# Two layers of a transformer kernel with another order of each engine's work

## The reference

```python
q = rmsnorm(x @ Wq + bq, qn_w)            # per head
k = rmsnorm(ctx @ Wk + bk, kn_w)          # per head
v = ctx @ Wv + bv
p = softmax(q @ k.T * scale + mask)
out = (p @ v) @ Wo
```

```python
q, k, v = linear_fp8(x, wq), linear_fp8(x, wk), linear_fp8(x, wv)   # own
qx = linear_fp8(x, wqx)                                            # asks the context
kx, vx = split(ctx @ w_kv_x)
q, k, qx, kx = (layernorm per head of each)
core = softmax(q @ k.T * scale) @ v
xout = softmax(qx @ kx.T * scale) @ vx
out = round_fp8(concat(core, xout) / smooth) @ wproj
```

## Time and profile before

| | us |
|---|---|
| median of three runs | 4422.85 (4418.86 to 4425.76) |
| the profiled execution | 4422.6 |
| its span, first to last instruction | 4420.8 |
| `l2x`, tiles 0 to 6 | 392.7 |
| `l2x`, last tile | 47.6 |
| `l3x`, one period | 97.5 |

### The profile page before, as it was taken

How to read it: one execution, slowest core, us unless ns; L and a number is a source line. 1 busy time by engine, 2 the same in 40 slices (tenths; PEclk the granted TensorE clock), 3 DMA queues, 4 the chain that set the end, 5 groups by cost and what they waited for, 6 DMA issues and landing times. The chain is left out here.

```text
span 4420.8 us, 69997 instructions
## 1 busy us (share of the span) xinstructions
PE 3591.5 (81%) x26672; PEld 2566.4 (58%) x26672; DVE 2633.6 (60%) x5418; ACT 1722.9 (39%) x3305; POOL 361.6 (8%) x566
## 2 busy tenths in 40 slices
PE   7999998997787887753888776878888886878778
PEld 4655557876764555531555643535555555757667
DVE  6888885443367777876444363247667665453552
ACT  4888883111344343421333212224444442223323
POOL 3000000000000000000111000111111111121000
PEclk8555558998886666756988788989999997989787
DMA  2000001000010000010000014000000001200000
GB/s 78 1 0 0 0 0 72 0 0 19 7 36 20 0 0 0 0 58 2 5 5 5 5 59 134 0 3 3 3 5 3 3 3 35 82 0 0 1 1 10
DMA packets 44826, 72.66 MB, mean 16 GB/s; under 512 B 25805, under 2 KB 33489, under 8 KB 41045
## 3 DMA queue, kind: packets, MB, share of 16 engines
q1 hardware_dynamic: 36440, 70.54, 4.6%
q10 hardware_dynamic: 8256, 0.52, 0.2%
HBM read 67.91 MB, written 3.15 MB: 16 GB/s over the span
## 5 line engine op out<-in xcount | busy, mean ns | idle before, releaser
L1316 DVE TENSOR_SCALAR_CACHE_REDUCE l0x_ex<-l0x_s_ps 128x1024 f32<-128x1024 f32 x258 | 305.6, 1222 | 63.4 <-PE l0x_s_ps L1019 62.4
L1151 ACT ACTIVATE l0x_ex<-l0x_ex,l0x_neg_max,l0x_q_scale 128x2048 f32<-128x2048 f32 x128 | 267.9, 2093 | 52.4 <-DVE l0x_neg_max L1322 50.7
L1031 PEld LDWEIGHTS l0x_t_ps<-l0x_identb,l0x_pb 128*128 128x128 bf16 x2048 | 200.0, 142 | 109.4 <-issue 56.8
L1019 PE MATMUL l0x_s_ps<-l0x_kT,l0x_qT 64*128 64x512 bf16 x516 | 235.5, 600 | 32.9 <-ACT l0x_qT L1146 19.5
L1158 ACT ACTIVATE l0x_pt<-l0x_t_ps 128x1024 bf16<-128x1024 bf16 x256 | 246.3, 1014 | 32.2 <-PE l0x_t_ps L1031 32.2
L1031 PE MATMUL l0x_t_ps<-l0x_identb,l0x_pb 128*128 128x128 bf16 x2048 | 233.7, 304 | 6.8 <-ACT l0x_pt L1158 4.1
L1331 DVE TENSOR_SCALAR l0x_pb<-l0x_ex 128x2048 bf16<-128x2048 f32 x128 | 156.4, 1222 | 0.0
L263 PE MATMUL l3x_bank<-l3x_wproj,l3x_cat 128*128 128x256 f32 x512 | 120.7, 390 | 32.1 <-DVE l3x_cat L3345 32.1
L263 PE MATMUL l3x_bank<-l3x_w_kv_x,l3x_ctxT 128*128 128x512 f32 x256 | 129.8, 655 | 0.9 <-ACT l3x_ctx_q L762 0.9
L263 PEld LDWEIGHTS l3x_bank<-l3x_wproj,l3x_cat 128*128 128x128 f32 x512 | 96.1, 193 | 52.4 <-DVE l3x_cat L3345 38.7
L1019 PEld LDWEIGHTS l0x_s_ps<-l0x_kT,l0x_qT 64*128 64x128 bf16 x516 | 50.0, 121 | 129.4 <-issue 80.4
(11 more groups left out here) (740 smaller groups left out, 8651.6 us busy)
## 6 DMA issues: line engine op xcount, KB each, us to landing
l3x_wproj<-in_L_xattn_wproj SPq DMA_DIRECT2D x1, 4096.0 KB, 22.5
l3a_w<-in_L_attn_W SPq DMA_DIRECT2D x4, 1024.0 KB, 11.4
l2f_w<-in_L_ffn_w SPq DMA_DIRECT2D x1, 2816.0 KB, 12.4
l0x_ctxT<-in_ctxT SPq DMA_DIRECT2D x8, 256.0 KB, 3.0
l0a_wq<-in_L_attn_W_Q SPq DMA_DIRECT2D x1, 2048.0 KB
l0a_wk<-in_L_attn_W_K SPq DMA_DIRECT2D x1, 2048.0 KB
l0a_wv<-in_L_attn_W_V SPq DMA_DIRECT2D x1, 2048.0 KB, 8.0
l0a_wo<-in_L_attn_W_O SPq DMA_DIRECT2D x1, 2048.0 KB, 13.0
```

Source lines behind the costliest of these rows:

```text
L1019: ins = mm(s_ps[:, j * 512:(j + 1) * 512], qT[rows, h // 2, :], kT[rows, h // 2, j * 512:(j + 1) * 512], start=True, stop=True)
L1031: ins = nc.tensor.transpose(t_ps[:, j * P:(j + 1) * P], pb[:, h % 2, j * P:(j + 1) * P], identb[:])
L1151: s.activation(ex[:, h % 4, :], ex[:, h % 4, :], ACT.Exp, scale=q_scale[:, h:h + 1], bias=nb[:, h:h + 1], accum_out=sums[:, h:h + 1]).then ...
L1316: v.tensor_scalar(ex[:, h % 4, c], s_ps[:, c], 1.0, None, ALU.mult, ALU.max, accum_out=mx[:, h, half:half + 1]).then_inc(o.up(scores_taken ...
```

## The change

In both layers instructions change their places in the queues of TensorE, ScalarE, VectorE and GpSimd. None is added or removed. In `l2x` the first `mix` moves ahead of the turning of `q0`, the copies of turned probabilities ahead of the normalising that stood before them, and on VectorE `weigh(0)` ahead of `shift(1)` and the statistics of the queries ahead of `weigh(1)` and of `take_out(0)`. In `l3x` the opening of a tile becomes a function `begin`, called once before the loop and then for the next tile between the last two products; the loop's body now begins with turning `x0`. `x0.stats_of` and `own.shift` are likewise done for the first tile ahead of VectorE's loop, and for the next tile ahead of `add_out`. Within the period fills of the context's keys and values move ahead of `mix` and `turn` of the own attention, and the first product behind `cross.score(0)`.

```diff
--- before.py
+++ after.py
@@ -2759,8 +2759,9 @@
                 if more:
                     free(kk, t + 1)
                     q1.fill(pe, t + 1)
+                att.mix(pe, t, 0)
+                if more:
                     q0.turn(pe, t + 1)
-                att.mix(pe, t, 0)
 
                 att.turn(pe, t, 1)
                 if more:
@@ -2793,21 +2794,22 @@
                     whole(norm.scalar(o, ln_bank))
                     kk.normalise(o)
                     o.t = t
-                att.exponential(o, 1)
                 if more:
                     o.t = t + 1
                     kk.take(o)
-
+                    o.t = t
+                att.exponential(o, 1)
+                att.take_turned(o, 0)
+                if more:
+                    o.t = t + 1
                     q0.normalise(o)
+                    q0.take(o)
                     o.t = t
-                att.take_turned(o, 0)
+                att.take_turned(o, 1)
                 if more:
                     o.t = t + 1
-                    q0.take(o)
-
                     q1.normalise(o)
                     o.t = t
-                att.take_turned(o, 1)
                 act.wait_ge(att.out_ps.sem, att.out_ps.value(t))
                 if more:
                     o.t = t + 1
@@ -2879,18 +2881,18 @@
                     whole(normalising)
                     kk.stats_of(o)
                     o.t = t
+                att.weigh(o, 0)
                 att.shift(o, 1)
-                att.weigh(o, 0)
-                att.weigh(o, 1)
                 if more:
                     o.t = t + 1
                     q0.stats_of(o)
                     o.t = t
-                att.take_out(o, 0)
+                att.weigh(o, 1)
                 if more:
                     o.t = t + 1
                     q1.stats_of(o)
                     o.t = t
+                att.take_out(o, 0)
                 att.take_out(o, 1)
                 dve.wait_ge(y_ps.sem, y_ps.value(t))
                 v.tensor_tensor(xt, xt, y_bank, ALU.add).then_inc(o.up(tile_done), 1)
@@ -3445,43 +3447,45 @@
             free(sq0, 0)
             sv.fill(pe, 0)
             sq1.turn(pe, 0)
-            def tile(t, more):
+
+            def begin(t):
                 free(sq1, t)
                 x0.fill(pe, t)
                 pe.wait_ge(cross.out_taken.sem, cross.out_taken.value(t, 0))
                 own.score(pe, t, 0)
-
                 free(sv, t)
                 x1.fill(pe, t)
+
+            begin(0)
+            def tile(t, more):
                 x0.turn(pe, t)
-                if more:
-                    whole(ln.tensor(pe, t + 1, ln_bank))
-
                 free(x0, t)
                 pe.wait_ge(ctx_loaded.sem, ctx_loaded.value(t))
                 kc0.fill(pe, t)
                 if more:
+                    whole(ln.tensor(pe, t + 1, ln_bank))
+                x1.turn(pe, t)
+                if more:
                     pe.wait_ge(ln.ready.sem, ln.ready.value(t + 1))
                 pe.wait_ge(tile_done.sem, tile_done.value(t, 0))
                 own.turn(pe, t, 0)
-                x1.turn(pe, t)
-                own.mix(pe, t, 0)
 
                 free(x1, t)
                 kc1.fill(pe, t)
+                own.mix(pe, t, 0)
                 own.turn(pe, t, 1)
                 kc0.turn(pe, t)
-                own.mix(pe, t, 1)
 
                 free(kc0, t)
                 vc0.fill(pe, t)
+                own.mix(pe, t, 1)
                 kc1.turn(pe, t)
-                part_of_y(t, 0)
 
                 free(kc1, t)
                 vc1.fill(pe, t)
                 pe.wait_ge(own.out_taken.sem, own.out_taken.value(t))
                 cross.score(pe, t, 0)
+                part_of_y(t, 0)
 
                 free(vc0, t)
                 if more:
@@ -3512,6 +3516,8 @@
                     sv.fill(pe, t + 1)
                     sq1.turn(pe, t + 1)
                 part_of_y(t, 2)
+                if more:
+                    begin(t + 1)
                 part_of_y(t, 3).then_inc(y_ps.sem, 1)
             with pe.Fori(0, TILES - 1) as t:
                 tile(t, True)
@@ -3528,18 +3534,17 @@
             sv.take(first)
             def tile(t, more):
                 o = Order(act, L.order["act"], t)
-                own.exponential(o, 0)
-
                 x0.normalise(o)
                 x0.take(o)
+                own.exponential(o, 0)
+
+                x1.normalise(o)
                 if more:
                     o.t = t + 1
                     whole(ln.scalar(o, ln_bank, scale=ln_w, bias=ln_b))
                     o.t = t
-
-                x1.normalise(o)
+                x1.take(o)
                 own.take_turned(o, 0)
-                x1.take(o)
 
                 kc0.normalise(o)
                 own.take_turned(o, 1)
@@ -3592,9 +3597,12 @@
                 if more:
                     o.t = t + 1
                     whole(norm.pool(o))
+                    o.t = t
+                x1.invert(o)
+                if more:
+                    o.t = t + 1
                     whole(ln.pool(o))
                     o.t = t
-                x1.invert(o)
                 kc0.invert(o)
                 kc1.invert(o)
                 if more:
@@ -3657,15 +3665,16 @@
             round_inputs(first)
             for phase in (sk, sq0, sq1):
                 phase.stats_of(first)
+            x0.stats_of(first)
+            own.shift(first, 0)
             def tile(t, more):
                 o = Order(dve, L.order["dve"], t)
-                x0.stats_of(o)
                 if more:
                     o.t = t + 1
                     first_norm, second_norm = norm.vector(o, tile_of(env.x, t + 1)), ln.vector(o, norm.y[:])
                     next(first_norm)
                     o.t = t
-                own.shift(o, 0)
+                x1.stats_of(o)
                 if more:
                     o.t = t + 1
                     whole(first_norm)
@@ -3677,16 +3686,13 @@
                     whole(second_norm)
                     o.t = t
 
-                x1.stats_of(o)
+                kc0.stats_of(o)
                 if more:
                     o.t = t + 1
                     round_inputs(o)
                     o.t = t
-
-                kc0.stats_of(o)
+                kc1.stats_of(o)
                 own.take_out(o, 0)
-
-                kc1.stats_of(o)
                 own.take_out(o, 1)
                 dve.wait_ge(own.out_taken.sem, own.out_taken.value(t, 1))
                 round_heads(o, 0)
@@ -3718,6 +3724,11 @@
                 round_heads(o, 0)
                 dve.wait_ge(cross.out_taken.sem, cross.out_taken.value(t, 2))
                 round_heads(o, 1)
+                if more:
+                    o.t = t + 1
+                    x0.stats_of(o)
+                    own.shift(o, 0)
+                    o.t = t
                 dve.wait_ge(y_ps.sem, y_ps.value(t))
                 add_out(o, tile_done)
                 dve.wait_ge(o.sem, o.at())
```

More of the change, by code:

```diff
@@ L2799, in tile @@
                     kk.take(o)
-                    q0.normalise(o)
                     o.t = t
+                att.exponential(o, 1)
                 att.take_turned(o, 0)
@@ L2805, in tile @@
                     o.t = t + 1
+                    q0.normalise(o)
                     q0.take(o)
+                    o.t = t
+                att.take_turned(o, 1)
+                if more:
+                    o.t = t + 1
                     q1.normalise(o)
                     o.t = t
-                att.take_turned(o, 1)
                 act.wait_ge(att.out_ps.sem, att.out_ps.value(t))
```

## The result

Four runs of the changed kernel took 4273.82 us in the median (4268.19 to 4278.6), beside 4423.5 us (4418.86 to 4425.76) for the kernel before on the same chip: a ratio of 0.966, with a 95% interval of 0.9644 to 0.9675. The forecast was 4305 with a range of 4281 to 4350.

What follows compares the result with a forecast made beforehand. TensorE's own work was taken as the bound underneath, with waits and slow clock on top. From 4422.6 us, -98.7 in `l2x` and -19 in `l3x` gave 4305, range 4281 to 4350.

Steps and rivals of the forecast that it cites:

- the waits of 1.88 and 4.53: In each `l2x` period, TensorE's waits in us before `att.turn(0)` and `att.mix(1)`, forecast to go.
- the margins ahead of `mix(0)` and `mix(1)`: In `l2x`, time in hand before the two products start, forecast at 1.3 and 2.5 us.
- The last tile: In `l2x`, the tile with no next one to prepare: left at 47.6 us, between -4 and +2.
- Rival 4: In `l2x`, full clock not granted to a TensorE that never pauses: +181 us, 4585; chance 0.04.
- Rival 2: In `l2x`, one queue comes late after all: 25 us (4330) or 63 us (4368); chance 0.14.
- The jump's stall: In `l3x`, 4.7 us a period after VectorE's jump to the loop's head, taken as gone because the head moves past a block's edge.
- the new waits for `kc0.take` and `kc1.take`: In `l3x`, new TensorE waits before `vc0.fill` and `vc1.fill`: 1.7 and 1.2 us a period.
- the term for the clock: In `l3x`, clock expected to fall after the 5.1 us wait as before: 5 us a period kept, 5.3 in the sum.
- The ends of `l3x`: In `l3x`, the first tile, whose jump never stalled, -3 us and the last -2.
- Rival 1: In `l3x`, the loop's stall stays, on the way to the norm: 99.8 us a period, total 4335; chance 0.17.
- Rival 3: In `l3x`, the norm's wait shorter and the clock kept: 92.5 us a period, total 4288; chance 0.08.
- bound of -40 for `l3x`: The `l3x` gain's far bound in us, with clock loss and the wait for the norm both half.

Runs made afterwards that it cites:

- e8: The changed kernel with VectorE's queue of `l2x` put back as before, TensorE and ScalarE as after: 4298.76 us, ratio 0.9719.
- e3: The kernel before with ten small VectorE memsets in front of the `l3x` loop and nothing else changed: 4402.0 us, ratio 0.9947.
- e4: The changed kernel with 97 small VectorE memsets in front of the `l3x` loop: 4279.78 us, ratio 0.9678.
- e7: The changed kernel with 109 small VectorE memsets in front of the `l3x` loop: 4301.0 us, ratio 0.9721.
- e10: The changed kernel with `x1`'s statistics ahead of `add_out`, `own.weigh(0)` behind the norm's `y`, and `x1.turn`, `x1.take`, `kc1.fill` earlier in `l3x`: 4267.58 us, ratio 0.9643.
- e11: e10 with TensorE's wait for the norm's copies moved behind `kc1.fill` in its `l3x` queue: 4265.07 us, ratio 0.9654.
- e6: The changed kernel with TensorE's queue of `l2x` put back (`q0.turn` ahead of `mix(0)`), VectorE and ScalarE as after: 4320.71 us, ratio 0.9769.

## Why the prediction was right in its waits and wrong in its size

**`l2x`, -98.7 forecast, -110.1 measured.** Each step held: the waits of 1.88 and 4.53 gone, the margins ahead of `mix(0)` and `mix(1)` 1.5 and 2.5 us for 1.3 and 2.5, only the gaps ahead of the norm's turning and of the output product left, clock 1.00. The term was mis-sized: 42 us taken where 41.6 had been worked out and 40.93 came (gaps 0.95 for 1.2, work 40.0 for 40.3), 7.7 us over the first seven tiles. The last tile, left at 47.6 with bounds of -4 and +2, took 43.9. Rival 4, a clock not granted to a TensorE without pauses, is refuted by the 1.00 over 286 us. Rival 2 did not happen, but its price, 25 us for a gap of 1.88, is near what e8 showed for a gap of 1.9: 22 us in the layer.

**`l3x`, -19 forecast, -38.2 measured: the step that failed.** The jump's stall went for the reason given. e3, e4 and e7 show that the place decides, under both orders. `y` came 9.96 us after the sum for 10.0, TensorE's wait was 4.7 for 5.1, the new waits for `kc0.take` and `kc1.take` together 2.7 for 2.9, for `x0.take` 1.2 for 1.0. All waits add to 12.0, forecast 12.4. What failed is the term for the clock, "I keep its 5 us", 5.3 in the sum. It made 77.4 + 5.3 = 82.7 us of TensorE time, and it was 79.98. That is 2.7 of the 3.1 us by which 95.1 missed 92.0, and six periods of 3.1 are 18.6 us, nearly the whole difference of the layer.

The runs show two faults in that term. First, it was not consistent: before, the clock fell twice a period, for 6.7 us behind the 5.7 us wait and for 3.5 us behind the waits of 1.6 and 0.74 at 3184. The forecast removed these later waits from the sum and kept the slow clock that followed them. After, there is one slow stretch. Second, the term was made as period x (1 - clock), which counts slow time in which TensorE had nothing to do. What the slow clock costs is read from the same matmuls at either clock. The slow stretch of the changed kernel:

```profile
3149.22 0.69 PE L241 MATMUL l3x_bank<-ident,l3x_ln_y 128*128 128x128 f32 x2 [4.72 <-DVE l3x_ln_y L213]
3149.70 1.91 PE L707 MATMUL l3x_bank<-ident,l3x_rows 128*128 128x128 f32 x8
3151.41 1.91 PE L821 MATMUL l3x_bank<-ident,l3x_pb 128*128 128x128 f32 x8
3153.11 4.58 PE L263 MATMUL l3x_bank<-l3x_w_kv_x,l3x_ctxT 128*128 128x512 f32 x8
```

The same work in e10 at a clock of 1.00:

```profile
3238.27 1.04 PE L707 MATMUL l3x_bank<-ident,l3x_rows 128*128 128x128 f32 x8
3239.14 0.38 PE L241 MATMUL l3x_bank<-ident,l3x_ln_y 128*128 128x128 f32 x2
3241.30 3.67 PE L263 MATMUL l3x_bank<-l3x_w_kv_x,l3x_ctxT 128*128 128x512 f32 x8 [1.77 <-ACT l3x_ln_yT L255]
```

And in the kernel before, a fill in the first slow stretch, the wait of 1.6, and the `mix` in the second slow stretch:

```profile
3176.90 4.94 PE L263 MATMUL l3x_bank<-l3x_w_kv_x,l3x_ctxT 128*128 128x512 f32 x8
...
3184.31 0.66 PE L707 MATMUL l3x_bank<-ident,l3x_rows 128*128 128x128 f32 x4 [1.60 <-ACT l3x_rows L755]
...
3186.68 3.54 PE L831 MATMUL l3x_bank<-l3x_pt,l3x_own_v 128*128 128x128 f32 x16 [0.32 <-ACT l3x_pt L845]
```

The four groups of the changed kernel take 9.1 us for 6.1 at full clock (the turning of the probabilities takes 1.04 there, like that of the rows). So the slow clock cost about 3.0 us after, and its work is 77.0, near the 77.4 of the forecast: of the 5.3 about 3.0 came. Before, the same way of counting gives 4.1 (with two turnings of 1.12 for 0.66, and 1.95 for this `mix` at full clock), not 4.9. In e7 the clock of the period is 0.95, as before, and TensorE is busy for 79.09: the first three groups take the same time as above, but `kc1.fill` is back at 3.69, so some 2.1 us were lost where 95.58 x 0.05 gives 4.8. Most of the slow stretch lay in the 9.2 us wait.

**The ends of `l3x`** gave -6.7 us together, forecast -5. **Rival 1**, the stall stays, is e7: 95.6 a period and 4301, where the rival said 99.8 and 4335; it had the mechanism, but kept the same clock term. **Rival 3** had the number for a period, 92.5, by a way that was half right: less was lost to the clock, but the wait for the norm was no shorter (4.7). The rule of the Trainium skill (Runtime: NRT & Kernel Launch, Instruction fetch mechanics), two blocks of 256 instructions, and a taken branch out of them stalls, is borne out in its second half by e7. Its blocks are not: the packets here were 8 KB (5 packets, 0.04 MB), 128 instructions apart, and a body of some 269 stayed loaded in e3, e4 and after. How many instructions stay loaded in all was not measured. The reading of it that this loop stalls wherever it lies is refuted.

**What no step had:** `l3a` took 4.7 us more (361.0 for 356.3), by its clock; its instructions are the same. It did so too with the `l3x` part alone (361.0) and with e3's ten memsets (360.4), but not with the `l2x` part alone (356.6) nor in e11 (356.6), and in e4 it took 364.6. So it is not the new order of `l3x` alone that brings it. Why the clock fell otherwise was not tried and stays open.

So -117.7 forecast, and 11.4 more in `l2x`, 19.2 more in `l3x`, 4.7 given back in `l3a`: 143.6 of the profiled executions' 144.0. The medians are 149.7 apart; the 6 us between lie within the scatter of the changed kernel's executions, 4268.19 to 4278.6. Neither miss alone would have left the range: 4422.6 - 110.1 - 19 is 4293.5, and 4422.6 - 98.7 - 38.2 is 4285.7. The forecast's own bound of -40 for `l3x` held; its range had no room for a gain in `l2x` beside it.

Some sums of the prediction are slightly off, and nothing hangs on them: its rows give 4.9 for the clock where it adds 5.3, 40.3 + 1.2 is 41.5, and in rival 1 15 less 5 is 10, not 11. Its 3.42 us of stall after the sum was not all stall either, as e3 shows: 1.15 of it is a wait for `x0.fill` that stays in the old order.

## What to carry to other kernels

When a wait is taken out of a sum, take out the slow clock behind it as well, and price the clock from the same matmuls in a slow stretch and at full clock, not from the mean clock of a period. Before a stall at a loop's jump is laid to the order of the work, put a few idle instructions in front of the loop, in more than one number: if it goes, it is a matter of place, and any later edit ahead of the loop can bring it back. When an engine waits for a chain that starts at the end of the period, look for pieces of the chain that can run in the idle time ahead of that end.

## What the runs showed of the hardware

- VectorE's loop of some 269 instructions ran without a packet of instructions in its periods with 97 memsets put in front of it (e4), and with five packets and 4.5 us of stall a period with 109 (e7).
- In e6 the same wait of 2.1 us was followed by a slow clock in five periods of six and by none in the sixth (47.9 and 43.1 us); in e8 a wait of 1.9 us cost 1.7 us more in four periods of six.
- In the changed kernel's `l2x` TensorE kept a clock of 1.00 over 286 us in which it was busy for 279.8.
- The same eight 128x128 turnings took 1.91 us at a clock of 0.50 and 1.04 at 1.00.
